# Selective scan of an eight-layer kernel: two of eight dt*x*B pairs by TensorE diagonals, sums by transposing passes, D*x through the same accumulation

## The reference

```python
def step(h, inp):
    x_t, dt_t, B_t, C_t = inp
    dA = jnp.exp(dt_t[..., None] * A)
    dBx = dt_t[..., None] * B_t[:, None, :] * x_t[..., None]
    h = dA * h + dBx
    y = jnp.einsum('bdn,bn->bd', h, C_t)
    return (h, y)
...
dt = jax.nn.softplus(dt + dt_bias[None, :, None])
ys = _selective_scan(xc, dt, A, Bm, Cm)
y = (ys + D_param[None, :, None] * xc) * jax.nn.silu(z)
return jnp.einsum('bdl,hd->blh', y, out_proj_w)
```

## Time and profile before

| | us |
|---|---|
| runs | 5362.31, 5360.51, 5357.15; median 5360.51 |
| profiled execution, its own time | 5354.56 |
| its span, first to last instruction | 5352.8 |
| scan stage in it | from about 2376 to 4260, 64 items |

### The profile page before, as it was taken

How to read it: one execution, slowest core, us unless ns; L and a number is a source line. 1 busy time by engine, 2 the same in 40 slices (tenths; PEclk the granted TensorE clock), 3 DMA queues, 4 the chain that set the end, 5 groups by cost and what they waited for, 6 DMA issues and landing times. The chain is left out here.

```text
span 5352.8 us, 40461 instructions
## 1 busy us (share of the span) xinstructions
PE 4902.7 (92%) x14496; PEld 2349.2 (44%) x14496; DVE 3251.4 (61%) x3534; ACT 1881.3 (35%) x2677; POOL 2309.7 (43%) x1219
## 2 busy tenths in 40 slices
PE   8998989999868899968789999999999999999998
PEld 4443234467536444423333444444444344457443
DVE  1663468756457322239999999999999722103522
ACT  1554620045322111125555555555555410002100
POOL 1003420000022000019999999999999742100421
PEclk8899999999989999989999999999999999999999
DMA  2001030000010121142116436444644320000001
GB/s 75 1 1 67 32 118 24 28 17 1 9 34 1 40 68 67 50 123 53 42 40 174 133 124 179 140 133 134 181 140 124 127 82 0 24 0 27 22 16 47
DMA packets 180006, 360.84 MB, mean 67 GB/s; under 512 B 21790, under 2 KB 56734, under 8 KB 175710
## 3 DMA queue, kind: packets, MB, share of 16 engines
q1 hardware_dynamic: 171742, 330.45, 20.4%
q0 software_dynamic: 8064, 27.80, 1.4%
HBM read 300.50 MB, written 57.67 MB: 67 GB/s over the span
## 5 line engine op out<-in xcount | busy, mean ns | idle before, releaser
L2851 POOL TENSOR_TENSOR l2scan_h<-l2scan_dtx,l2scan_Bb 128x1024 f32<-128x1024 f32 x512 | 1198.2, 2358 | 30.8 <-DMA l2scan_Bb<-l_bc 15.0
L2753 PE MATMUL l2scan_yp<-l2scan_h,ident 128*128 128x512 f32 x2048 | 971.5, 608 | 115.1 <-POOL l2scan_h L2876 101.1
L2820 ACT ACTIVATE l2scan_ring<-l2scan_dt,l2scan_A 128x512 f32<-128x512 f32 x1024 | 663.9, 681 | 639.4 <-DVE l2scan_h L2932 481.0
L2753 PEld LDWEIGHTS l2scan_yp<-l2scan_h,ident 128*128 128x128 f32 x2048 | 389.3, 193 | 639.4 <-issue 481.1
L2743 PE MATMUL l2scan_low_z<-state,l2scan_Wz 128*128 128x512 f32 x1024 | 476.6, 598 | 0.3
L2876 POOL TENSOR_TENSOR l2scan_h<-l2scan_h,l2scan_Cb 128x1024 f32<-128x1024 f32 x192 | 452.1, 2355 | 8.6 <-DVE l2scan_h L2921 0.9
L2411 PE MATMUL l2in_acc<-state,l2in_W 128*128 128x512 f32 x1024 | 444.9, 595 | 10.5 <-DMA l2in_W<-l_attn_in_x 10.5
L2932 DVE TENSOR_TENSOR l2scan_h<-l2scan_ring,l2scan_Cb 128x1024 f32<-128x1024 f32 (+1 forms) x384 | 394.3, 1041 | 6.1 <-DMA l2scan_Cb<-l_bc 0.7
L2921 DVE TENSOR_TENSOR_SCAN l2scan_ring<-l2scan_ring,l2scan_carry,l2scan_h 128x512 f32<-128x512 f32 x320 | 392.7, 1273 | 0.0
L2921 DVE TENSOR_TENSOR_SCAN l2scan_ring<-l2scan_ring,l2scan_h 128x512 f32<-128x512 f32 x320 | 373.3, 1212 | 5.5 <-POOL l2scan_h L2851 5.5
L2538 PE MATMUL l2scan_oacc<-l2scan_oy,l2scan_oW 128*128 128x512 f32 x768 | 353.1, 592 | 0.0
(11 more groups left out here) (409 smaller groups left out, 7538.2 us busy)
## 6 DMA issues: line engine op xcount, KB each, us to landing
l2scan_oy<-l_y SPq DMA_DIRECT2D x192, 512.0 KB, 4.9
l2scan_Wz<-l_attn_in_z SPq DMA_DIRECT2D x64, 512.0 KB, 3.6
l2scan_oW<-l_attn_out_w SPq DMA_DIRECT2D x192, 128.0 KB, 3.3
l_xc<-l2in_xc SPq DMA_DIRECT2D x16, 1024.0 KB, 4.8
l2scan_xc<-l_xc SPq DMA_DIRECT2D x64, 256.0 KB, 5.7
l2scan_Bb<-l_bc SPq DMA_DIRECT2D x128, 128.0 KB, 6.9
l2scan_Cb<-l_bc SPq DMA_DIRECT2D x128, 128.0 KB, 7.8
l_y<-l2scan_zs SPq DMA_DIRECT2D x64, 256.0 KB, 5.5
```

The source lines that it names most:

```text
L2753: last = t.matmul(yp[:, :], K.ident[:, :], h[:, st % SLOTS, j, :], start=g == 0 and j == 0, stop=g == NSG - 1 and j == SGR - 1)
L2820: a.activation(bank(st, j), dt[:, q % 2, :], ACT.Exp, scale=A[:, ct, n:n + 1]).then_inc(dA_ok, 1)
L2851: g_.tensor_tensor(h[:, st % SLOTS], dtx[:, None, :].to_broadcast([P, SGR, NT]), Bb[:, g * SGR:(g + 1) * SGR, :], ALU.mult).then_inc(dBx_o ...
```

## The change

- `MAKERS` = PPTPPPTP: at g = 2 and g = 6 TensorE makes dBx. ScalarE copies B's columns once a chunk and makes 16 diagonal matrices of them (`diagonals`); per item TensorE transposes dtx (`turn_dtx`), ScalarE copies it (`keep_dtx`), and TensorE multiplies the transposed dtx with the diagonals (`spread`) straight into a PSUM pair. In these steps the decay goes to the SBUF slot of `h`.
- `KINDS` = YWYWYWYW: GpSimd multiplies by C in four steps of eight instead of three.
- The PSUM ring of five banks becomes two pairs, used by Y steps alone. The decay of W steps goes to a new SBUF buffer `dAw` of two pairs. So in a W step both inputs of the scan, decay and dBx, lie in SBUF.
- `total` sums with transposing passes, four of 128x128 for each product, into `yT`; D*x is made by ScalarE (`skip`) and added in the same accumulation (`add_skip`). ScalarE copies the sum to SBUF (`keep`), TensorE turns it back (`turn_back`), and VectorE's `finish`, now at g = 2, only multiplies by the gate.
- `ssm` has one buffer instead of two, `Bb` holds 12 rows instead of 16, the projection's ring two pieces instead of three.

```diff
-KINDS = "YWYWYWYY"
+KINDS = "YWYWYWYW"
+MAKERS = "PPTPPPTP"
...
-        self.RING = 3
+        self.RING = 2
...
-        ring = s.ps("ring", [P, BANKS, NT])
...
+        dAw = s.sb("dAw", [P, PAIRS, SGR, NT])
+        ring = s.ps("ring", [P, PAIRS, SGR, NT])
+        yT = s.ps("yT", [P, BLOCKS, P])
...
-                    if ct == 1 and c and c + 1 < CHUNKS:
+                    if ct == CT - 2 and c + 1 < CHUNKS:
...
+                        t.wait_ge(copied, q)
+                    for j in range(SGR):
+                        for k in range(BLOCKS):
+                            last = t.matmul(yT[:, k, :], h[:, st % SLOTS, j, k * P:(k + 1) * P], K.ident[:, :], is_transpose=True,
+                                            start=g == 0 and j == 0 and k == 0, stop=g == NSG - 1 and j == SGR - 1 and k == BLOCKS - 1)
...
+                def turn_dtx(q):
+                    t.wait_ge(dtx_ok, q + 1)
...
+                        last = t.transpose(yp[:, k * P:(k + 1) * P], dtx[:, k * P:(k + 1) * P], K.ident[:, :])
+                    last.then_inc(dx_ready, 1)
+
+                def spread(st):
+                    q, g = divmod(st, NSG)
+                    n = made("T", st)
+                    t.wait_ge(dg_ok, q // CT + 1)
+                    t.wait_ge(dx_ok, q + 1)
+                    wait_pair(t, st)
+                    for j in range(SGR):
+                        i = SGR * MAKERS[:g].count("T") + j
+                        for k in range(BLOCKS):
+                            last = t.matmul(bank(st, j)[:, k * P:(k + 1) * P], dtxT[:, k, :], dg[:, i, k, :], start=True, stop=True)
+                    last.then_inc(dBxT_ok, 1)
+
+                def add_skip(q):
+                    t.wait_ge(skip_ok, q + 1)
+                    for k in range(BLOCKS):
+                        last = t.matmul(yT[:, k, :], u[:, k * P:(k + 1) * P], K.ident[:, :], is_transpose=True, start=False, stop=False)
+                    last.then_inc(skipped, 1)
+
+                def turn_back(q):
+                    t.wait_ge(copied, q + 1)
+                    t.wait_ge(dx_ok, min(q + 2, ITEMS))
+                    if q:
                         t.wait_ge(y_ok, q)
-                    for j in range(SGR):
-                        last = t.matmul(yp[:, :], K.ident[:, :], h[:, st % SLOTS, j, :], start=g == 0 and j == 0, stop=g == NSG - 1 and j == SGR - 1)
-                    last.then_inc(summed, 1)
+                    for k in range(BLOCKS):
+                        last = t.transpose(yp[:, k * P:(k + 1) * P], ysb[:, k, :], K.ident[:, :])
+                    last.then_inc(turned_back, 1)
...
+                    if g == 2 and q:
+                        turn_back(q - 1)
...
+                    if st + 1 < STEPS and maker(st + 1) == "T":
+                        spread(st + 1)
...
+                def keep(q):
+                    a.wait_ge(summed, (q + 1) * NSG)
+                    a.wait_ge(dt_ok, min(q + 2, ITEMS))
+                    if q:
+                        a.wait_ge(turned_back, q)
+                    a.activation(ysb[:, :, :], yT[:, :, :], ACT.Copy).then_inc(copied, 1)
+
+                def skip(q):
+                    ct = q % CT
+                    a.wait_ge(c_ok, min(q + 2, ITEMS))
+                    a.wait_ge(l_ok, min(q + 2, ITEMS))
+                    a.wait_ge(dtx_ok, q + 1)
+                    a.activation(u[:, :], xc[:, q % 3, :], ACT.Copy, scale=Dp[:, ct:ct + 1]).then_inc(skip_ok, 1)
...
+                def keep_dtx(q):
+                    a.wait_ge(dx_ready, q + 1)
+                    if q:
+                        a.wait_ge(dBxT_ok, made("T", q * NSG - 1))
+                    a.activation(dtxT[:, :, :], yp[:, :].rearrange("p (k d) -> p k d", d=P), ACT.Copy).then_inc(dx_ok, 1)
+
+                def diagonals(c):
+                    a.wait_ge(bt_ok, c + 1)
+                    if c:
+                        a.wait_ge(dBxT_ok, made("T", c * CT * NSG - 1))
+                    for g in range(NSG):
+                        if maker(g) == "P":
+                            continue
+                        for j in range(SGR):
+                            i, n = SGR * MAKERS[:g].count("T") + j, g * SGR + j
+                            for k in range(BLOCKS):
+                                last = a.activation(dg[:, i, k, :], K.ident[:, :], ACT.Copy, scale=BT[:, k, n:n + 1])
+                    last.then_inc(dg_ok, 1)
...
+                    if maker(st) == "P":
+                        wait_pair(a, st)
+                        decay = ring[:, pair(st)] if kind(st) == "Y" else dAw[:, pair(st)]
+                    else:
+                        if st >= SLOTS:
+                            a.wait_ge(summed, st - SLOTS + 1)
+                        decay = h[:, st % SLOTS]
                     for j in range(SGR):
                         n = g * SGR + j
-                        wait_bank(a, st, j)
-                        a.activation(bank(st, j), dt[:, q % 2, :], ACT.Exp, scale=A[:, ct, n:n + 1]).then_inc(dA_ok, 1)
+                        a.activation(decay[:, j, :], dt[:, q % 2, :], ACT.Exp, scale=A[:, ct, n:n + 1]).then_inc(dA_ok, 1)
                     if g == 1 and q:
+                        keep(q - 1)
...
+                        if maker(st) == "T":
+                            dA, dBx = hs[:, j, :], bank(st, j)
+                        else:
+                            dA, dBx = bank(st, j) if kind(st) == "Y" else dAw[:, pair(st), j, :], hs[:, j, :]
+                        last = v.tensor_tensor_scan(out, dA, dBx, init, ALU.mult, ALU.add)
...
-                    if g == 1 and q:
+                        v.tensor_tensor(hs, ring[:, pair(st)], Cb[:, g * SGR:(g + 1) * SGR, :], ALU.mult).then_inc(hC_v, 1)
+                    if g == 2 and q:
```

More of the change, by code:

```diff
@@ L2583, in l2_scan @@
         xc_in = [s.sem(f"xc_in{j}") for j in range(3)]
-        ssm_in = [s.sem(f"ssm_in{j}") for j in range(2)]
+        ssm_in = s.sem("ssm_in")
         c_in = [s.sem(f"c_in{g}") for g in range(NSG)]
@@ L2606, in upto, with made, rows_at @@
             return q * KINDS.count(k) + KINDS[:g].count(k)
+        def made(k, st):
+            q, g = divmod(st + 1, NSG)
+            return q * MAKERS.count(k) + MAKERS[:g].count(k)
+        def rows_at(g):
+            at = SGR * MAKERS[:g].count("P")
+            return slice(at, at + SGR)
         def carries(k, st):
@@ L2618, in wait_hC, with pair, wait_pair @@
                 e.wait_ge(hC_g, upto("W", st))
+        def pair(st):
+            return (upto(kind(st), st) - 1) % PAIRS
         def bank(st, j):
[L2621 to L2635, removed]
+            return ring[:, pair(st), j, :]
+        def wait_pair(e, st):
+            k = kind(st)
+            n = upto(k, st) - PAIRS
+            if n <= 0:
+                return
+            if k == "Y":
+                e.wait_ge(hC_v, n)
+            else:
+                e.wait_ge(h_ok, max(i for i in range(st) if kind(i) == "W" and upto("W", i) == n) + 1)
         with nc.Block() as block:
@@ L2732, in dt_tile @@
                         t.wait_ge(dt_ok, q)
-                    t.matmul(low_z[:, :], Wdt[:, q % 2, :], ssm[:, c % 2, :], start=True, stop=True).then_inc(dt_ready, 1)
+                    t.matmul(low_z[:, :], Wdt[:, q % 2, :], ssm[:, :], start=True, stop=True).then_inc(dt_ready, 1)
                 def z_part(q, k0, k1):
@@ L2766, in _ @@
                         dt_tile(q + 1)
+                    if g == 4 and q + 1 < ITEMS and (q + 1) % CT == 0:
+                        turn_rows((q + 1) // CT)
+                    if g == 6 and q + 1 < ITEMS:
+                        turn_dtx(q + 1)
                     if g == 5:
@@ L2774, in _ @@
                 total(STEPS - 1)
+                turn_back(ITEMS - 1)
             @block.scalar
@@ L2826, in _ @@
                         log1p(q + 1)
+                        if (q + 1) % CT == 0:
+                            columns((q + 1) // CT)
+                    if g == 5:
+                        skip(q)
+                    if g == 7 and q + 1 < ITEMS:
+                        keep_dtx(q + 1)
+                        if (q + 1) % CT == 0:
+                            diagonals((q + 1) // CT)
+                keep(ITEMS - 1)
                 gate(ITEMS - 1)
@@ L2925, in _ @@
                         if first(q):
-                            for js, src in runs(st):
-                                last = v.tensor_copy(carry[:, ct, g * SGR + js.start:g * SGR + js.stop], src[:, :, NT - 1])
-                            last.then_inc(carried_v, 1)
+                            v.tensor_copy(carry[:, ct, g * SGR:(g + 1) * SGR], ring[:, pair(st), :, NT - 1]).then_inc(carried_v, 1)
                         if ct == 0:
                             v.wait_ge(c_in[g], 16 * COPIES * (c + 1))
-                        for js, src in runs(st):
-                            last = v.tensor_tensor(hs[:, js], src, Cb[:, g * SGR + js.start:g * SGR + js.stop, :], ALU.mult)
```

(4 more changed lines are left out.)

79 lines of the change are left out of this document (63 added, 16 removed).

## The result

The changed kernel takes 5702.5 us (median of 4 runs, 5697.2 to 5709.8) against 5358.9 for the kernel before, measured beside it: ratio 1.0641, 95% interval 1.0623 to 1.0660. The forecast was 5775 with a range of 5640 to 5960. The profiled execution took 5709.8 us; its own counterpart in the forecast is 5770.

A forecast was written before the change was run, and what follows sets the result against it. POOL's work and two-SBUF W scans, unable to overlap, bound the item: 26.1 + 9.2 = 35.3 us. (35.3 - 28.93) x 64 = 408, plus 7, on 5354.6 gives 5770; the median 6 above, 5775 us, range 5640 to 5960.

The forecast's parts named there:

- The step that decides: W scans with two SBUF inputs and POOL's work exclude each other, so an item takes 26.1 + 9.2 = 35.3 us.
- The first rival: In the W steps, scans do not exclude POOL; DVE then sets the item and the time is 5244 us; chance 0.05.
- the second: No exclusion, and the wait behind `keep` shows: a stall of 1.8 to 4.1 us an item, 5327 to 5475; chance 0.04.
- The size of the hold: Each W scan holds POOL 1.04 us, its record less 0.23 as seen at `L2019`; 9.2 us an item with waits.
- my lower bound, 0.88: Hold per W scan taken as the share 0.52 / 0.753 of its record; gives 33.1 us an item, 5635 in all.
- The waits of the C product: At g = 1, 3, 7 POOL's C product waits for its pair's second scan and a semaphore: 1.32 us each.
- POOL and DVE alternate as walked: Walk through W steps g = 1, 3, 5, 7: DVE takes 35.5 us; POOL lacks work only under a scan.
- The fourth rival: Every W step waits half a product, then a whole one, with POOL idle between: 40.4 us an item, 6100; chance 0.10.
- The sign that I gave for it: POOL showing several us of idle an item that ends on DVE would mean the bad alternation holds.
- POOL's records near the whole stage: Sign for the forecast: POOL's records, and DVE's too, would fill nearly the whole scan stage.
- `keep` was covered: Chain from W7's end through `keep` and gate to step 2's scan: 7.9 us against DVE's 9, or 6.1 without exclusion.
- The third rival: PE's clock in the scan falls and PE becomes the bound; at a granted 0.67 together 6066 us; chance 0.08.

The follow-up runs named there:

- run two: The kernel before with only its W decays moved to an SBUF buffer and the projection's ring cut to two pieces: 5708.8 us, ratio 1.0659.
- run one: The changed kernel with the W decays back in PSUM, all steps sharing the two pairs, so no scan has two SBUF inputs: 5443.1 us, ratio 1.0164.
- run four: As run one, with the gate ahead of `keep` on ScalarE and `keep` a step later: 5339.2 us, ratio 0.9964.
- run five: The changed kernel, decays in SBUF, with only the gate put ahead of `keep` and `keep` a step later: 5705.7 us, ratio 1.0655.
- runs eight and nine: Eight: run four with TensorE's dBx steps at g=1 and 5 and `spread` issued first, 5318.1 us; nine: eight with gate product at g=3, 5308.2 us.

## Why the prediction was right, and where a term was off

**The step that decides held.** The W scans read two SBUF inputs, and this is enough for the loss: run two adds that to the kernel before, with a projection ring that costs nothing there, and loses 350 us; run one takes it away and gains 259, and the other 84, with 20 more, went with the reorder of run four. The first rival (scans do not exclude POOL) is dead by the 3.3 us scans; the second is what run one shows, with 5443 in its 5327 to 5475.

The prediction said that the trace has one place where DVE reads two SBUF inputs beside a POOL product. It has at least one more, in the same stretch and with the same outcome. Four small products of `l1ffn_p` and `l1ffn_row`, both in SBUF, begin at 1643.53 beside one POOL product, run on beside the next, and take 3.71 us together. At 1600.60, with POOL idle, they took 0.50:

```profile
L1825 DVE TENSOR_TENSOR l1ffn_kept<-l1ffn_p,l1ffn_row x16: 177/184/2329, 1571.2 to 1699.2; 128x32 f32<-128x32 f32 x16
...
1643.53 3.71 DVE L1825 TENSOR_TENSOR l1ffn_kept<-l1ffn_p,l1ffn_row 128x32 f32<-128x32 f32 x4
1644.80 2.38 POOL L168 TENSOR_TENSOR l1ffn_sq<-l1ffn_sq 128x1024 f32<-128x1024 f32 x1
```

**The size of the hold was off.** The failing term is "A scan holds POOL for 1.27 - 0.23 = 1.04 us by that row". The rows show 0.91 to 0.93 where one dBx product meets one scan (g = 7 and 1), and less at g = 5. I had carried the 0.23 over from a short instruction as a constant. As a share it does better: 0.52 / 0.753 is 0.69 of the record, 0.92 / 1.27 is 0.72; these are two instructions, not a rule. The share was the source of my lower bound, 0.88, and the value lies nearer to that than to 1.04. The waits of the C product were 1.16 instead of 1.32, since I added a whole record where the start-to-start distance of scans, 2.44 / 2 = 1.22, was at hand. And g = 5 cost 1.43 where I had two full holds, 2.08; its first scan held POOL partly during the gap of 0.23 that is there anyway. Together 7.9 instead of 9.2, and the gap, which the sum had left out, takes 0.2 back. Over 64 items 35.3 - 34.45 makes 54 of the 60 us between 5770 and the profiled 5709.8.

**The Trainium skill's sentence** ("SBUF — State Buffer", "Who interferes with whom"), that the first of the two has the port pair for the whole instruction while the other fully blocks, agrees with this trace on the block. Read as the whole record, it would have given 5840 us. The measured hold is 0.92 us of a 1.27 us record, so the whole record overstates it, as my 1.04 did by less.

**POOL and DVE alternate as walked.** W3 has both scans in succession (2.91), W7 a stretched product between them (4.65), and so on. The fourth rival (bad alternation, 6100) needed POOL out of work for 5 us beside the waits of the forecast; apart from waits for scans it has nearly none. The sign that I gave for it, several us of POOL's idle an item that end on DVE, can't tell the two apart: the profile shows 294 / 64 = 4.6 us of just that, and the forecast's own sum contained it (the first scan of g = 3 and three times 1.32, 5.0 us). For the same reason "POOL's records near the whole stage" was a wrong sign: they fill 85% of it.

**`keep` was covered**, by run five, and would show without the exclusion, by run one. Both halves of that paragraph held, the second with 3.9 us inside its 1.8 to 4.1.

**PE, ACT.** The 16 diagonals took 4.77 us at the start, priced at 5. Eight transposes take 1.04 us as a group, the last's latency included, as in the earlier trace rows:

```profile
2385.21 4.77 ACT L2933 ACTIVATE l2scan_dg<-ident,l2scan_BT 128x128 f32<-128x128 f32 x16
...
3403.88 1.04 PE L2777 MATMUL l2scan_yT<-ident,l2scan_h 128*128 128x128 f32 x8
```

PE's clock did fall in chunk 0, to a granted 0.83 where PE is busy 70% of the time, and stood at 0.98 in chunk 1. The third rival needed PE to become the bound; at 0.83 its 19.8 us an item are 24, and the item takes over 34. So by this sum the clock cost nothing; no run holds it apart.

**The gain that did not show** is real but small. On engine counts everything shrank to about 27 us; with the exclusion gone, the best order found gives 28.1 and 0.9% over the kernel before. The rest seems to be in PE, though no run takes work from it: it is busy 95%, and two of its new duties (dBx in time for DVE, the sum in time for `keep`) depend on its place in the queue.

What stays open: PE still waits some 50 us in runs eight and nine for the loads of `oy` into the ring of two pieces, where the kernel before had three. That ring was not restored, so its price is not known.
